# Capacity mixtures that choose their experts on the logits, sequence by sequence, with the softmax in one exponential beside the choice

## What is computed

```python
logits = x @ gate_w.T                          # E = 64 experts
scores = jax.nn.softmax(logits, axis=-1)
topk_w, topk_i = jax.lax.top_k(scores, K)      # K = 6
...
pos[...] = rank of the pair among the pairs of the same expert, in order of tokens
valid = pos < CAP                              # CAP = 32 slots for each expert
buf[flat_i, slot] = x[token_ids]
y = (silu(buf @ w_gate) * (buf @ w_up)) @ w_down       # for each expert
out = sum over k of y[flat_i, slot] * (topk_w * valid)
return out + (silu(x @ sw_gate) * (x @ sw_up)) @ sw_down   # shared expert
```

## Time and profile before

| | |
|---|---|
| median of 3 runs | 1851.41 us (1850.69 to 1851.79) |
| the profiled execution's own time | 1852.99 us |
| its span, first to last instruction | 1851.2 us |
| busy: PE, DVE, ACT, POOL | 1671.3, 1335.6, 1023.1, 660.0 us |
| opening of the first capacity mixture, from PE's first `shared` to PE's first spread of the loop | 1132.29 to 1175.96 |
| the same place of the second mixture, first `shared` matmul shown | 1674.82, PE's down from 1709.83 |
| last `sum_up` of the first and the second mixture | from 1299.87 and from 1842.47 |

### The profile page before, as it was taken

The page is one execution under the profiler, slowest core; times in us unless marked ns, Lnnn a source line. Parts: engine busy times, 40 slices in busy tenths (PEclk is TensorE's granted clock), DMA queues, the critical chain, the costliest instruction groups (busy, mean ns, idle before and its releaser), DMA issues.

```text
span 1851.2 us, 34297 instructions
## 1 busy us (share of the span) xinstructions
PE 1671.3 (90%) x10911; PEld 1346.0 (73%) x10912; DVE 1335.6 (72%) x2830; ACT 1023.1 (55%) x2200; POOL 660.0 (36%) x604
## 2 busy tenths in 40 slices
PE   3877999899999999989999989899699999897998
PEld 1223788777777988867777778677588888786776
DVE  7996777788886577777778755765688888756664
ACT  4654543478775454357777745211588788734111
POOL 1664320266663132026556530100355555421000
PEclk7998999999999999999999999999899999999999
DMA  1000220000001022000000033398011000033695
GB/s 62 2 1 23 71 69 1 12 18 20 20 11 35 18 80 67 1 12 24 23 14 23 4 125 95 117 255 241 24 29 28 28 29 23 0 125 95 179 257 151
DMA packets 34895, 111.51 MB, mean 60 GB/s; under 512 B 4992, under 2 KB 18544, under 8 KB 27888
## 3 DMA queue, kind: packets, MB, share of 16 engines
q1 hardware_dynamic: 32424, 92.96, 16.6%
q10 hardware_dynamic: 2376, 17.30, 3.4%
HBM read 109.19 MB, written 1.05 MB: 60 GB/s over the span
## 4 chain that ended last, share of the span: by engine, by line
PE 67%; DVE 18%; ACT 8%; issue 6%; ACTq 0%; DVEq 0%; DMA 0%; POOL 0%; SPq 0%; POOLq 0%
PE banks L1033 7%; PE banks L1009 4%; PE banks L1743 4%; PE banks L1679 3%; PE banks L583 3%; PE banks L585 3%; PE banks L584 3%; PE banks L988 3%; PE banks L989 2%; PE banks L990 2%; PE banks L1047 2%; PE banks L1048 2%; PE banks L940 2%; PE banks L1049 2%; PE banks L942 2%
## 5 line engine op out<-in xcount | busy, mean ns | idle before, releaser
L1457 POOL TENSOR_TENSOR xn<-xn 128x512 f32<-128x512 f32 x132 | 171.5, 1299 | 254.4 <-DVE xn L1341 254.4
L1443 POOL TENSOR_SCALAR prob<-prob,recip 128x256 f32<-128x256 f32 (+2 forms) x256 | 228.3, 906 | 69.4 <-DVE recip L1325 69.3
L1217 ACT ACTIVATE prob<-banks,peak 128x256 f32<-128x256 f32 (+3 forms) x384 | 190.2, 501 | 105.1 <-DVE peak L1316 96.0
L1033 PE MATMUL banks<-pt,v 128*128 128x256 f32 (+3 forms) x768 | 203.2, 407 | 6.9 <-ACT pt L1152 6.9
L1033 PEld LDWEIGHTS banks<-pt,v 128*128 128x128 f32 x768 | 143.6, 189 | 73.5 <-issue 33.0
L1316 DVE TENSOR_REDUCE peak<-banks 128x1 f32<-128x256 f32 (+3 forms) x384 | 161.5, 448 | 17.5 <-PE banks L992 15.8
L988 PE MATMUL banks<-k_hi,q_hi 128*128 128x256 f32 (+2 forms) x384 | 152.5, 397 | 21.2 <-DVE k_lo L1332 20.6
L1428 POOL TENSOR_TENSOR wq_lo<-wq,wq_hi 128x256 fp32r<-128x256 f32 x48 | 36.2, 754 | 317.7 <-ACT wq_hi L1167 317.7
L1009 PE MATMUL banks<-ident,prob 128*128 128x128 f32 x864 | 141.6, 281 | 3.2 <-DVE pt L1150 3.2
L681 POOL TENSOR_TENSOR w_parts<-raw,w_parts 128x768 fp32r<-128x768 f32 x36 | 67.2, 1867 | 157.8 <-ACT w_parts L637 157.8
L1341 DVE TENSOR_TENSOR xn<-xn,ropes 128x512 f32<-128x512 f32 x138 | 122.3, 886 | 0.0
(11 more groups left out here) (249 smaller groups left out, 5032.7 us busy)
## 6 DMA issues: line engine op xcount, KB each, us to landing
wgu<-in_w_gu SPq DMA_DIRECT2D x32, 1408.0 KB, 14.8
wd<-in_w_d ACTq DMA_DIRECT2D x24, 704.0 KB
raw<-in_w SPq DMA_DIRECT2D x36, 384.0 KB, 3.1
wd<-in_w_d SPq DMA_DIRECT2D x8, 704.0 KB
wkv<-in_mha_kv SPq DMA_DIRECT2D x16, 256.0 KB, 2.7
wq<-in_mqa_q SPq DMA_DIRECT2D x16, 128.0 KB, 2.0
wo<-in_mqa_o SPq DMA_DIRECT2D x16, 128.0 KB, 2.1
wq<-in_gqa_q SPq DMA_DIRECT2D x16, 128.0 KB, 2.0
```

What stands on the lines that cost most here:

```text
L1033: last = pe.matmul(o_bank[:, x * P:to], v[:, s, x, at:at + P], pt[:, s, x, first:first + to - x * P], start=(j == 0), stop=(j == NQ - 1))
L1217: last = act.activation(prob[:, s, cols[t]:cols[t] + n], s_bank[gi][:, psum_col[t]:psum_col[t] + n], ACT.Exp, bias=peak[:, s, t:t + 1], ac ...
L1443: last = pool.tensor_scalar(part, part, recip[:, s, t:t + 1], None, ALU.mult)
L1457: pool.tensor_tensor(cosed_at(i, m, r), cosed_at(i, m, r), swap[:, r % 2, :], ALU.add) \
```

## The change

Only `capacity_mixture` changes.

- **Logits by sequence.** `logits(0)` and `logits(1)` go to two banks; `logits(0)` now stands ahead of `shared(0)` on PE. `count_places` uses a third bank and stands ahead of `shared(4)` rather than behind it.
- **Choice on the logits.** DVE copies a sequence's logits to SBUF, finds the largest, subtracts the maximum into `wrest`, replaces the six largest by -3e38 and makes the mask. `choose(0)` stands behind the first product, `choose(1)` behind the second; the additions over the tiles are cut in two.
- **Softmax beside it.** ACT runs one exponential over all of `wrest` (128x512) behind `shared_high(2)`, with silu's table loaded back right behind it. DVE sums, inverts, masks and scales later.
- **First product.** `shared_product(0)` stands behind `norm.normalise(1)` on DVE, `shared_high(0)` behind `norm.parts_scalar(1)` on ACT.
- **Weights split.** The split into three parts and `x_lo` with `parted` stand behind `pairs` and `picks` on DVE.
- **The end.** The last `sum_up` signals `summed` a second time after its first four tiles, and DVE's first two additions wait for that one. ACT preloads the square root's table at the end where a stage follows.

```diff
@@ PE
         norm.wait_parts(pe, 0)
+        pe.wait_ge(c["loaded"].sem, 64)
+        logits(0)
         pe.wait_ge(c["sw_low"].sem, 1)
         shared(0)
-        pe.wait_ge(c["loaded"].sem, 64)
-        logits(0)
...
         shared(3)
+        count_places()
         shared(4)
-        count_places()
         shared(5)
...
+                if isinstance(i, int) and i == LOOPS and n == BODY - 1 and t == NT // 2 - 1:
+                    last.then_inc(c["summed"].sem, 1)
@@ ACT
         shared_silu(0)
+        norm.parts_scalar(act, 1)
         shared_high(0)
-        norm.parts_scalar(act, 1)
-        shared_silu(1)
-        shared_high(1)
-        act.wait_ge(c["peak"].sem, 1)
-        for t in range(NT):
-            last = act.activation(score[:, t, 0:NE1], banks[:, 0, t * NE1:(t + 1) * NE1], ACT.Exp,
-                                  bias=peak[:, t:t + 1], accum_out=sums[:, t:t + 1])
-        last.then_inc(c["expd"].sem, 1)
-        for n in range(2, NSH * NSEQ):
+        for n in range(1, NSH * NSEQ):
             shared_silu(n)
...
             shared_high(n)
+            if n == 2:
+                act.wait_ge(c["peak"].sem, 1)
+                act.activation(wrest[:, :, :], wrest[:, :, :], ACT.Exp).then_inc(c["expd"].sem, 1)
+                act.preload_act_table(ACT.Silu)
...
+        if st.next:
+            act.preload_act_table(ACT.Sqrt)
@@ DVE
+        def choose(s):
+            cut, bank = slice(s * HT, (s + 1) * HT), banks[:, s, 0:HT * NE1].rearrange("p (t e) -> p t e", e=NE1)
+            dve.wait_ge(c["logits"].sem, s + 1)
+            link(dve.tensor_copy(score[:, cut, 0:NE1], bank))
+            for t in norm.tiles(s):
+                op = dve.max(top[:, t, :], score[:, t, 0:NE1])
+            link(op)
+            op = dve.tensor_tensor(wrest[:, cut, :], score[:, cut, 0:NE1],
+                                   top[:, cut, 0:1].broadcast_to([P, HT, NE1]), ALU.subtract)
+            if s == 1:
+                op.then_inc(c["peak"].sem, 1)
+            link(dve.memset(top[:, cut, TOP1:], SENTINEL))
+            for t in norm.tiles(s):
+                op = dve.match_replace(left[:, t, :], top[:, t, :], score[:, t, :], FLOOR)
+            link(op)
+            link(dve.tensor_scalar(maskb[:, cut, :], left[:, cut, 0:NE1], FLOOR / 2, None, ALU.is_lt))
...
-        shared_product(0)
         norm.normalise(dve, 1)
         norm.wait_xn(dve)
+        shared_product(0)
+        choose(0)
         norm.parts_vector(dve, 1)
+        count_ahead(1, HT + 1)
         shared_product(1)
+        choose(1)
+        count_ahead(HT + 1, NT)
         shared_product(2)
         shared_product(3)
 ...
+        dve.wait_ge(c["expd"].sem, 1)
+        link(dve.reduce_sum(sums[:, :], wrest[:, :, :], axis=AX.X))
+        link(dve.reciprocal(sums[:, :], sums[:, :]))
         shared_product(4)
...
         shared_product(5)
...
         pairs(0, 0, 0)
         pairs(0, 0, 1)
         picks(0, 0)
+        split_weights()
+        rest_of_tokens()
         slot(0, -1)
...
-        wait(dve, c["summed"], NG1)
         for t in range(0, NT, 2):
+            wait(dve, c["summed"], NG1 + t // (NT // 2))
```

More of the change, by code:

```diff
@@ L1612, in logits @@
                 for kc in range(NC):
[L1613 removed]
+                    last = pe.matmul(banks[:, s, t % HT * NE1:(t % HT + 1) * NE1], g.xt[:, kc, t * P:(t + 1) * P],
                                      router[:, kc, :], start=(kc == 0), stop=(kc == NC - 1))
@@ L1620, in count_places @@
             for t in range(NT):
-                pe.matmul(banks[:, 1, t * NE1:(t + 1) * NE1], ranks[:, 0:P], maskb[:, t, :], start=True, stop=False)
-                last = pe.matmul(banks[:, 1, t * NE1:(t + 1) * NE1], ranks[:, P:], ahead[:, t, :],
+                pe.matmul(banks[:, 2, t * NE1:(t + 1) * NE1], ranks[:, 0:P], maskb[:, t, :], start=True, stop=False)
+                last = pe.matmul(banks[:, 2, t * NE1:(t + 1) * NE1], ranks[:, P:], ahead[:, t, :],
                                  start=False, stop=True)
@@ L1888, in _, with count_ahead @@
+        def count_ahead(first, beyond):
+            for t in range(first, beyond):
+                op = dve.tensor_tensor(ahead[:, t, :], ahead[:, t - 1, :], maskb[:, t - 1, :], ALU.add)
+                if t < NT - 1:
+                    link(op)
+            if beyond == NT:
+                op.then_inc(c["masked"].sem, 1)
         norm.normalise(dve, 1)
         norm.wait_xn(dve)
+        shared_product(0)
+        choose(0)
         norm.parts_vector(dve, 1)
+        count_ahead(1, HT + 1)
@@ L1891, in _ @@
         shared_product(1)
[L1892 to L1896, removed]
-        link(dve.tensor_tensor(score[:, :, 0:NE1], score[:, :, 0:NE1],
-                               sums[:, :].unsqueeze(2).broadcast_to([P, NT, NE1]), ALU.mult))
-        for t in range(NT):
-            op = dve.max(top[:, t, :], score[:, t, 0:NE1])
@@ L1903, in _ @@
-        link(op)
-        link(dve.memset(top[:, :, TOP1:], SENTINEL))
+        choose(1)
+        count_ahead(HT + 1, NT)
         shared_product(2)
-        for t in range(NT):
-            op = dve.match_replace(left[:, t, :], top[:, t, :], score[:, t, :], -1.0)
-        link(op)
         shared_product(3)
-        dve.tensor_scalar(maskb[:, :, :], left[:, :, 0:NE1], 0.0, None, ALU.is_lt)
-        link(dve.scalar_tensor_tensor(wrest[:, :, :], left[:, :, 0:NE1], 0.0, score[:, :, 0:NE1],
-                                      ALU.is_lt, ALU.mult))
@@ L1914, in _ @@
-        for t in range(1, NT):
-            op = dve.tensor_tensor(ahead[:, t, :], ahead[:, t - 1, :], maskb[:, t - 1, :], ALU.add)
-            if t < NT - 1:
-                link(op)
-        op.then_inc(c["masked"].sem, 1)
-        link(dve.tensor_copy(wpart[:, :, :], wrest[:, :, :]))
-        dve.tensor_copy(wparts[:, :, :, 0], wpart[:, :, :])
-        link(dve.tensor_tensor(wrest[:, :, :], wrest[:, :, :], wpart[:, :, :], ALU.subtract))
-        link(dve.tensor_copy(wpart[:, :, :], wrest[:, :, :]))
@@ L1942, in picks, with rest_of_tokens @@
+        def rest_of_tokens():
+            dve.wait_ge(c["xpart"].sem, 1)
+            dve.tensor_tensor(x_lo[:, :, :], g.xn[:, :, :], x_hi[:, :, :].bitcast(F32), ALU.subtract) \
+                .then_inc(c["xrest"].sem, 1)
+            dve.wait_ge(c["xrest"].sem, 1)
+            dve.sem_inc(c["parted"].sem, 1)
         def picks(i, m):
```

29 lines of the change are left out of this document (17 added, 12 removed).

## The result

| | before | after |
|---|---|---|
| median | 1851.25 us (5 runs, 1844.93 to 1851.79) | 1835.78 us (5 runs, 1834.72 to 1837.73) |
| profiled execution | 1852.99, span 1851.2 | 1837.73, span 1835.8 |
| first opening | 1132.29 to 1175.96: 43.67 | 1131.66 to 1170.37: 38.71 |
| second opening | 1674.82 to 1718.58: 43.76 | 1666.75 to 1705.45: 38.70 |

The ratio is 0.9927, 95% interval 0.9915 to 0.9938: faster, by 15.5 us where 11.0 were forecast; 1835.78 lies just above the lower end of the range. An opening is now counted from PE's first logits matmul, which, as the first `shared` matmul did before, opens PE's work on the normalised first sequence.

What follows compares the result with a forecast made beforehand. Product 5's date on DVE was taken to set the opening. Two openings of 4.4 plus ends of 1.0 and 1.2 gave 11.0, from the median of 1851.41 to 1840.4; the 8-in-10 range was 1835.5 to 1845.

Steps and rivals of the forecast that it cites:

- Product 5 some 27 after the start: Sign in the opening: product(5) starts some 27 after PE's first logits matmul, instead of 34.2 after its first shared one.
- step 1: Opening's start, logits and normalisation first: PE's wait of 1.35 goes, clock expected to stay up, product(0) at 1137.6.
- Steps 2 to 5: Choice of both sequences, exponential, then product(3) to product(5): product(5) at 1159.5, 7.0 earlier than 1166.48 with the preceding part.
- step 6: Split and `parted` behind the one-hots: 12.05 from product(5), PE waits about 2.6, leaving a gain of 4.4 an opening.
- the early choice does nothing: Rival: product(5) gains only the 2.6 that `parted` takes, leaving 2.2 from the ends, 1849.2; chance 3%.
- The wait for `parted`, 2.6: Sign on PE between down and the first spread: a new wait of some 2.6 for x_lo; far from that, forecast fails.
- The clock in PE's new waits: Rival: PE's clock falls in its new waits, making shared(5) and the first gather some 2 longer each; 1848.4, chance 4%.
- Races: `place` and the scaling start 0.1 ahead of POOL's operation; rival losing both: 2 x 1.25 an opening, 1845.4, chance 9%.
- Holds: POOL's operations hold DVE's mask, subtraction, `pairs` and x_lo; without any holds, together 3.8, an opening would give 8.2.
- The rival without holds: Rival: POOL's holds don't bite, falling on replacements, maxima and products; gain 16.2, 1835.2, chance 18%.
- Table loads: ACT's exponential: each load 1.28 without the page's drain, otherwise the sum is 5.5; rival of double cost: 1845.5, chance 4%.
- The ends: Ends of both mixtures: first additions no longer wait for the other 8 matmuls; 1.0 at the first, 1.2 at the second.

Runs made afterwards that it cites:

- the front: Kernel before with only logits(0) ahead of shared(0) and the normalisation ahead of the first product, its high half behind the normalisation's parts: 1839.15 us, ratio 0.9926.
- the repeat: The changed kernel run again, unaltered, beside two refitted kernels on one chip: 1837.98 us, ratio 0.9936.
- the ends alone: Kernel before with only the last sum's signal after its first four tiles, and the first two additions waiting for it: 1847.05 us, ratio 0.9974.
- the refit: Changed kernel with DVE's work reordered: product(2) earlier, x_lo ahead of product(3), scale and split behind the first one-hots; x_hi, shared(4) earlier: 1831.63 us, ratio 0.99.
- filled waits: Refitted order with PE's two waits filled by unread matmuls: 1829.69 us; with the weights' mask also moved behind the one-hots and fewer fills: 1828.21 us.
- the run with the early split: Changed kernel with the weights' split ahead of product 5 and x_lo right behind it: 1848.97 us, ratio 0.9993.

## Why the prediction was right, point by point

- **Product 5 some 27 after the start**: 26.99, 7.2 earlier where 7.0 were forecast. Products 1 to 4 lie within 0.25 of the working too (11.82, 16.69, 21.92 and 24.94 after the start, forecast 11.9, 16.9, 22.1 and 25.1). DVE's wait of 4.55, the two loads and the exponential on ACT, and POOL's two holds in the choice stood where the working had them.
- **Which step earns it**: this the prediction did not see. It summed steps 1 to 5 and never asked what step 1 gives alone. Moving the normalisation ahead of the first product brings down's start forward by 5.5 of the 7.2, and shortens the opening by 5.5, more than the 5.0 of the whole change. Steps 2 to 5 give product 5 another 1.5 to 1.7, and step 6 takes 2.2 back. On top of the front, the rival "the early choice does nothing" was therefore true of the opening's length, though it was priced as if without the choice there were no gain: the front was inside it. Without the front the choice, softmax and split do give 1.9 and 3.1.
- **The wait for `parted`, 2.6**: 0.60 was measured, and by the prediction's own sign (a wait far from 2.6) this step failed. Its cost was nearly right, its place wrong: `parted` lets PE go on 11.7 after product 5 (12.05 forecast), but down took 10.4 rather than 8.74, because the clock fell there. The loss is 10.98 - 8.74 = 2.24; with the clock held at 1.00 it stands as a bare wait of 2.12.
- **The clock in PE's new waits** (4%): it did fall, over down's start in both openings, and in part 5 in the repeat. Its price of 4 an opening was wrong, since PE waits for `x_lo` at down's end: nothing in the first profile, 0.7 in the repeat. The argument that rested on one stretch at 1164 to 1166, where PE was thinly busy and the clock stayed up, did not carry.
- **Races**: `place` won by 0.11, the scaling by 0.10 (1157.92 against 1158.02). In the second opening the leads were 0.11 and 0.10 again, and neither was held there.
- **Holds**: confirmed, but the opening without them is 2.1 to 2.4 shorter and not 3.8, since other things then set part of it: in the first opening down takes 10.22 at a lower clock, and in the second product 5 waits 1.04 for ACT's silu. The rival without holds had 1835.2, close to the median, and was still wrong.
- **Table loads**: silu starts 0.01 after its load ends, the load 0.02 after the exponential. The page "ScalarE: Activation LUTs" of the Trainium skill, section "What ACT_TABLE_LOAD costs", has the load's 1283 ns right; its drain of about 1380 ns shows in none of these rows, and the sum without it was the right one.
- **The ends**: 0.96 for 1.0 at the first. At the second 2.27 for 1.2: the signal gives 1.4, the rest is that the sum of before ran at the low clock and that of after didn't. The term was taken from the length of two of DVE's additions; what counts is that the additions now start behind 8 matmuls, and the four together are as long as before (2.48).
- **The rest, 2.2**, is in stages whose code nothing changes: 0.63 ahead of the first opening, 1.55 in the attention between the mixtures. Over the kernels run here, with the same code there, that attention stretch (statistics behind the first mixture to the second opening) takes 368.8 to 371.8, and the first opening starts between 1128.0 and 1134.7. Before had 371.53 and 1132.29, after 369.99 and 1131.66, the repeat of after 368.80 and 1132.10. The kernel before and the one with the ends alone have 371.53 and 371.69 there, but the changed kernel with its split moved has 371.80, so whether the change itself shortens that stretch stays open. The change's own part of the 15.5 is about 12 to 13. That the time fell inside the range, 0.3 above its lower end, is partly luck: the sum of 11.0 was 1 to 2 too small, and these 2.2 came on top.

## What to carry to other kernels

Sum a change by its parts, and price each part alone before summing: here one move on DVE and one on ACT, with four normalisations ahead of one product, gave the whole gain of the opening, while the large rewrite beside it gained on one result and gave that back in the wait it made. When a rewrite opens a wait on the engine that sets the end (here 4.55), look at once what queued work can go into it and what stands behind the last result that the next engine needs; in the refit, with `x_lo` moved there and the clock held up, that was worth 4.1 an opening, 1.9 by an earlier product 5 and 2.2 by PE's wait that went (the single moves were not run alone). Whether a low clock costs anything depends on what the engine waits for afterwards: fill the waits and see if the time moves.

## What the runs showed of the hardware

- Three kinds of DVE instruction from SBUF to SBUF ended 0.15 to 0.29 behind POOL's operation when they started while it ran: a mask (0.29 became 1.14), a subtraction (0.43 became 1.31) and, in the run with the early split, a cast (0.42 became 1.37). A match-replacement that ran beside the same POOL operation as the mask kept its 0.21. `place`, which began 0.11 ahead of POOL, was not held; POOL's operation then took 1.74 rather than 1.28.
- The granted clock over down differed between the two openings of one execution of the same code (the refit: 36.00 and 34.53, with the same dates to 0.05 up to down's start). With filled waits down took 8.73 to 8.74 in all four openings of the refitted order, as long as in the kernel before, where the clock was 1.00.
- The median of the kernel before moved from 1848.45 to 1851.25 between comparisons, and its single runs from 1844.5 to 1859.2, more than the three runs ahead of the prediction (1850.69 to 1851.79) suggest.
